# A fused four-layer graph network: layer 0's relu into a PSUM bank, compact means, and newly drawn instruction lists

## The chip, the cores and the metric

The kernel runs on one core of one Trainium2 chip. The time is that of one execution on the device, in microseconds (us), as the median of three runs. Five engines work side by side, each through its own queue in order: PE (TensorE, matmuls), DVE (VectorE), ACT (ScalarE), POOL (GpSimd) and SP (SyncE, which here only issues DMAs). They wait for each other by semaphores.

## What is computed

Four graph layers stand one behind the other, each with a layer norm and a relu ahead of it and a residual around it, for 128 graphs of 128 nodes with 256 features and one common adjacency matrix:

```python
h = jnp.maximum(_layernorm(x), 0.0)
x = x + _L0_gnn_ref(h, adj, W, b)          # deg * (h Wi' + b) + adj @ (h Wj')
h = jnp.maximum(_layernorm(x), 0.0)
x = x + _L1_gnn_ref(h, adj, W, a_src, a_dst)   # Wh, leaky-relu logits, masked softmax, attn @ Wh
h = jnp.maximum(_layernorm(x), 0.0)
x = x + _L2_gnn_ref(h, adj, W, a)          # as layer 1 with F1 = 128; out is [attn @ hW, hW]
h = jnp.maximum(_layernorm(x), 0.0)
x = x + _L3_gnn_ref(h, adj, Wq, bq, ...)   # 8-head masked attention and an output projection
```

In layers 1 and 2 a logit is e_src of one node plus e_dst of another; so each graph needs one column of 128 numbers (e_dst) as a row on all partitions.

## The kernel before, in words

Two graphs (a pair) are worked on at a time, 64 pairs in all, and everything of a pair stays on the chip. The kernel is a software pipeline, unrolled in full: each engine's function has a `step(t)` that lists its operations in a fixed order, and `LAG` gives for each operation by how many steps it runs behind. At step t an operation handles pair t - LAG. So `LAG`, together with the order of the `if due(...)` lines, is the whole schedule of an engine; within a step the order is the order of its queue. `BANKS` gives each matmul result one of the eight PSUM banks (2 KB per partition) and the operation that frees it; `bank_free` waits for whoever held that bank last by this order.

Products that need more than the fast format holds are made of a high and a low part: ACT rounds a tile (`..._hi`), DVE takes the difference (`..._lo`), and PE adds three products (L988 to L990). The operations that matter here:

- Layer 0. `xt` is the pair's x, transposed on the host and loaded by SP (L252). DVE makes mean and variance from x (`stats0`, `mv0`, L537, L551). SP writes the means to a small DRAM tensor (L259) and reads them back to all partitions (`mean_b`, L266); POOL subtracts them from xt (L380). ACT rounds the relu of that (`relu_difference_high`, L812), and DVE takes relu minus rounded (`relu_difference_low`, L591). PE multiplies (`project0`, L988 to L990), and multiplies by the adjacency (`aggregate`, L1024).
- Layer 1. POOL normalises (L388), PE transposes (`h1t`, L998), ACT and DVE make relu high and low (L803, L599), PE projects (`project1`), ACT copies the result (`wh`, L825). POOL gathers the e_dst column (`dst1`, L411), SP writes it (L278) and spreads it to all partitions (`db1`, L284). ACT's `sum_logits` (`z1`, L851) reads that row and writes leaky-relu logits into the upper half of bank 7; DVE masks (L609), ACT takes exps (L860), PE transposes (`e1t`, L1060), ACT copies (`at1`, L868), PE multiplies (`attend`, L1068).
- Layer 2 runs the same way with names that end in 2; its relu'd transpose is one copy (`relu_transposed2`, `ht2`, L831), its projection is `project2` (L1044) into `hh`, and its sum of logits (`z2`) uses the same bank 7. For the first four and last five pairs PE transposes the column in place of the DMAs.
- Layer 3: projections kt, qt, v, `scores` (L1105), exps (L882, four at a time), POOL's product with the inverse sums (L417), PE's transposes (L1113), ACT's copies (L890), `attend3` (L1125), and the output projection `project4`; DVE adds the residual (L675) and SP stores.

The places that the change and the prediction's steps touch:

```python
    "zz1": (7, "z1", ('nmax1',)),
    "zz2": (7, "z2", ('nmax2',)),
...
                act.wait_ge(row_in[i][p % 2], ((p - BY_TRANSPOSE[0]) // 2 + 1) * 16)   # sum_logits waits for the row's DMA
...
                passed(act, "h2t", p)                                                  # relu_transposed2
                passed(pe, "ht2", p)                                                   # project2
```

Of the kernel before, what the change touches and what calls it, by code (L numbers as in the profile page):

```python
# [13 lines left out]
P = 128  # L14
D = 256
# [32 lines left out]
    "m1": (1, "m1", ('mj_lo1', 't0_1')),  # L48
    "pt0": (3, "pt0", ('p3t_0',)),
    "x4b": (2, "x4_mm", ('x4',)),  # L50
    "m0": (5, "m0", ('mj_lo0', 't0_0')),
    "kt": (0, "kt_mm", ('kt',)),
    "d1": (4, "d1", ('z1',)),
    "at2": (6, "e2t", ('at2',)),
    "qt": (2, "qt_mm", ('qt',)),
# [1 line left out]
    "pt3": (0, "pt3", ('p3t_3',)),
    "x3b": (6, "x3_mm", ('x3',)),
    "h1t": (3, "h1t", ('h1t_lo',)),
    "hh": (2, "hh_mm", ('hh',)),  # L60
    "sc0": (4, "scores", ('nmax3_0',)),
    "sc1": (1, "scores", ('nmax3_1',)),
    "sc2": (5, "scores", ('nmax3_2',)),
    "sc3": (0, "scores", ('nmax3_3',)),
    "ot": (2, "ot_mm", ('ot_lo',)),
    "at1": (6, "e1t", ('at1',)),
    "h0t": (6, "h0t", ('d0s',)),
    "v": (3, "v_mm", ('v',)),
    "pt1": (6, "pt1", ('p3t_1',)),
    "x2b": (1, "x2_mm", ('x2',)),  # L70
    "x1b": (2, "s0", ('x1',)),
    "wh1": (5, "wh1_mm", ('wh1',)),
    "wh0": (3, "wh0_mm", ('wh0',)),
    "h3t": (0, "h3t", ('h3t_lo',)),
    "prep": (6, "products", ('w1_split',)),
    "pt2": (5, "pt2", ('p3t_2',)),
    "d2": (4, "d2", ('z2',)),
# [1154 lines left out]
```

## Time and profile before

| | |
|---|---|
| median of 3 runs (lowest, highest) | 1249.41 us (1247.36, 1253.91) |
| the profiled execution: time, span | 1256.04 us, 1254.0 us |
| PE, POOL, DVE, ACT busy | 1216.2, 1106.0, 1079.9, 1061.9 us |
| granted TensorE clock, mean | 0.996 |
| DMA | 86.76 MB, mean 69 GB/s |
| read from HBM, written | 66.92 MB, 17.02 MB |

Times in the profile are from the first instruction. Matmuls overlap each other, so a matmul's listed duration (0.28 us) is longer than the distance to the next one (0.12 us): distances between starts tell the pace. A wait is listed with the engine and line that waited, and behind the arrow with whoever released it. "PEld" is the load of a matmul's weights, which runs ahead of the matmul. With 64 pairs the first steps fill the pipeline and the last ones drain it.

### The profile page before, as it was taken

What the parts mean: (1) busy time and instruction counts of PE and PEld (TensorE: products, weight loads), DVE (VectorE), ACT (ScalarE), POOL (GpSimd) and SP (SyncE); (2) the same over time, 40 slices, a digit from 0 to 9 for tenths busy, and PEclk for the clock granted to TensorE, in tenths of its full rate; (3) what the DMA queues carried; (4) which work ended last, traced back from release to release, by engine and by line L of the source; (5) the groups of instructions that cost most, each with busy time, mean ns of one, the idle gap of its engine ahead of it and who ended that gap; (6) DMA issues with size and microseconds to landing.
All of it is one profiled execution on the core that took longest, in us unless ns stands there. A gap on an engine that the chain in (4) does not pass through costs nothing. (4 is left out here: it accounts for less than half of the span.)

```text
span 1254.0 us, 43654 instructions
## 1 busy us (share of the span) xinstructions
PE 1216.2 (97%) x12001; PEld 1117.9 (89%) x12001; DVE 1079.9 (86%) x5141; ACT 1061.9 (85%) x3911; POOL 1106.0 (88%) x1848
## 2 busy tenths in 40 slices
PE   7899999999999999999999999999999999999996
PEld 6689999999999889999999989999998999999996
DVE  5798988988988888988998988998988988988884
ACT  3578888898988888888998988898898898888996
POOL 5889989999999889999999989999999899998763
PEclk9999999999999999999999999999999999999999
DMA  6323434444443434435434444534435534431000
GB/s 181 83 48 48 82 60 75 82 66 69 83 65 69 82 57 77 77 66 74 82 64 71 79 60 78 81 59 76 79 64 74 83 57 78 80 55 31 19 20 35
DMA packets 97679, 86.76 MB, mean 69 GB/s; under 512 B 31649, under 2 KB 81313, under 8 KB 97441
## 3 DMA queue, kind: packets, MB, share of 16 engines
q1 hardware_dynamic: 94960, 82.26, 37.8%
q8 instruction: 102, 1.67, 0.6%
q14 instruction: 137, 1.11, 0.5%
q10 hardware_dynamic: 2480, 1.71, 0.5%
HBM read 66.92 MB, written 17.02 MB: 67 GB/s over the span
## 5 line engine op out<-in xcount | busy, mean ns | idle before, releaser
L882 ACT ACTIVATE exps<-masked,nmax 128x128 f32<-128x128 f32 x1024 | 397.0, 396 | 0.2 <-DVE nmax L652 0.2
L417 POOL TENSOR_TENSOR probs<-exps,rsum 128x512 f32<-128x512 f32 x256 | 274.8, 1075 | 22.1 <-DVE rsum L660 22.1
L652 DVE CUSTOM_DVE_ANT_0 masked<-bank,mask 128x128 f32<-128x128 f32 x1024 | 229.6, 285 | 11.4 <-ACT exps L882 7.3
L388 POOL TENSOR_SCALAR y<-x,nm,rstd 128x256 f32<-128x256 f32 x384 | 228.5, 604 | 1.9 <-issue 1.0
L882 ACT ACTIVATION_READ_ACCUMULATOR exps<-masked,nmax 128x1 f32 x1024 | 199.3, 195 | 0.0
L537 DVE BATCH_NORM_STATS2 stats<-x 128x6 f32<-128x256 f32 x512 | 188.6, 411 | 11.0 <-DMA x<-in_x 8.6
L365 POOL TENSOR_TENSOR rstd<-veps,power 128x2 f32<-128x2 f32 x256 | 183.1, 715 | 0.1
L988 PE MATMUL bank<-w_hi,ht_hi 128*128 128x512 f32 (+1 forms) x512 | 180.5, 352 | 0.9 <-DVE ht_lo L599 0.5
L989 PE MATMUL bank<-w_lo,ht_hi 128*128 128x512 f32 (+1 forms) x512 | 175.1, 342 | 0.0
L990 PE MATMUL bank<-w_hi,ht_lo 128*128 128x512 f32 (+1 forms) x512 | 174.8, 341 | 0.0
L1113 PE MATMUL bank<-ident,probs 128*128 128x128 f32 x1024 | 153.6, 273 | 0.3 <-ACT v L874 0.3
L890 ACT ACTIVATE probs3t<-bank 128x512 f32<-128x512 f32 x256 | 150.8, 590 | 2.4 <-PE bank L1113 2.3
L1113 PEld LDWEIGHTS bank<-ident,probs 128*128 128x128 f32 x1024 | 122.4, 142 | 8.7 <-issue 0.9
L998 PE MATMUL bank<-ident,y 128*128 128x128 f32 x768 | 116.6, 275 | 6.7 <-POOL y L388 6.7
L990 PEld LDWEIGHTS bank<-w_hi,ht_lo 128*128 128x128 f32 x512 | 97.0, 189 | 11.9
L988 PEld LDWEIGHTS bank<-w_hi,ht_hi 128*128 128x128 f32 x512 | 96.7, 189 | 11.3 <-DVE ht_lo L599 0.9
L989 PEld LDWEIGHTS bank<-w_lo,ht_hi 128*128 128x128 f32 x512 | 97.3, 190 | 9.3
L860 ACT ACTIVATE ez<-z,nmax 128x128 f32<-128x128 f32 x256 | 99.8, 395 | 2.2 <-DVE nmax L609 2.0
L998 PEld LDWEIGHTS bank<-ident,y 128*128 128x128 f32 x768 | 89.5, 142 | 9.1 <-POOL y L388 8.9
L380 POOL TENSOR_TENSOR xt_sb<-xt_sb,mean_b 128x512 f32<-128x512 f32 x62 | 96.9, 1562 | 0.0
L599 DVE SCALAR_TENSOR_TENSOR ht_lo<-bank,ht_hi 128x512 fp32r<-128x512 f32 x128 | 86.2, 673 | 11.2 <-ACT ht_hi L803 11.1
L825 ACT ACTIVATE wh<-bank 128x258 f32<-128x258 f32 x128 | 49.5, 387 | 50.4 <-PE bank L990 50.4
(129 smaller groups left out, 3904.9 us busy)
## 6 DMA issues: line engine op xcount, KB each, us to landing
x<-in_x SPq DMA_DIRECT2D x64, 256.0 KB, 5.7
xt_sb<-in_xt SPq DMA_DIRECT2D x64, 256.0 KB, 5.1
out<-x SPq DMA_DIRECT2D x64, 256.0 KB
mean_b<-rows SPq DMA_DIRECT2D x62, 256.0 KB, 4.4
db<-rows SPq DMA_DIRECT2D x110, 128.0 KB, 4.0
rows<-dst SPq DMA_DIRECT2D x110, 1.0 KB, 4.0
rows<-mv SPq DMA_DIRECT2D x62, 2.0 KB, 3.1
probs<-in_w0t ACTq DMA_DIRECT2D x1, 256.0 KB, 6.3
```

The lines of the kernel that those rows point to most:

```text
L365: pool.tensor_tensor(rstd[i][:, b], veps[i][:, b], power[:], ALU.pow).then_inc(S[f"rstd{i}"], 1)
L388: last = pool.tensor_scalar(y[i][:, b, g], src[:, bx, g], nm[i][:, s, g:g + 1], rstd[i][:, s, g:g + 1], ALU.add, ALU.mult)
L417: pool.tensor_tensor(probs3[:, p % BUFFERS["probs3"], j], exps3[:, p % BUFFERS["exps3"], j], rsum3[:, s, j].unsqueeze(2).to_broadcast([P, ...
L537: last = dve.bn_stats(stats[i][:, b, g], src[:, bx, g])
L652: last = dve.tensor_tensor_reduce(masked3[:, b, j, i], bank_of(f"sc{j}")[:, i * P:(i + 1) * P], mask[:], scale=-1.0, scalar=-MASKED, op0=A ...
L882: last = act.activation(exps3[:, b, j, i], masked3[:, p % BUFFERS["masked3"], j, i], ACT.Exp, bias=nmax3[:, s, j, i:i + 1], scale=-1.0, ac ...
L890: act.activation(probs3t[:, b, j].rearrange("p b n -> p (b n)"), bank_of(f"pt{j}")[:], ACT.Copy).then_inc(S[f"p3t_{j}"], 1)
L988: pe.matmul(out_ap, lhs[0], rhs[0], start=start, stop=False)
L989: pe.matmul(out_ap, lhs[0], rhs[1], start=False, stop=False)
L990: return pe.matmul(out_ap, lhs[1], rhs[0], start=False, stop=stop)
L998: last = pe.transpose(bank_of(f"h{i}t")[:, (c * G + g) * P:(c * G + g + 1) * P], y[i][:, b, g, c * P:(c + 1) * P], ident[:])
L1113: last = pe.transpose(bank_of(f"pt{j}")[:, i * P:(i + 1) * P], probs3[:, p % BUFFERS["probs3"], j, i], ident[:])
```

## The change

Four things are done.

1. **Layer 0's relu.** ACT writes the relu of the mean-free xt into bank 7 (new operation `h0r`), then copies that into `ht0_hi`, rounded; DVE subtracts the rounded part from the bank. So xt is read once, and its buffer is released by `h0r` alone. Bank 7 is shared in turn by `z1`, `h0r` and `z2`.
2. **The means.** `mv` holds the two graphs' means next to each other, and the two variances; only the means are written and spread, so the row is half as long, and POOL reads every second element instead of every fourth.
3. **Weights' semaphores.** Layer 3's weights for q, k and v count on one semaphore.
4. **The lists.** Order, lags and banks of all engines are drawn anew, with longer transfer times assumed.

```diff
 LAG = {
-       "adj_spread": -31, "m1": -6, "pt0": 1, "x4_mm": 2, "m0": -6, "kt_mm": -1, "d1": -4, "e2t": -2, "qt_mm": -1, "h2t": -3, "pt3": 1,
...
+       "adj_spread": -31, "pt0": 3, "pt3": 3, "d1": -2, "x3_mm": 0, "hh_mm": -1, "h1t": -3, "scores": 1, "ot_mm": 3, "h0t": -7, "v_mm": 1,
...
     "zz1": (7, "z1", ('nmax1',)),
+    "h0r": (7, "h0r", ('h0t_lo',)),
     "zz2": (7, "z2", ('nmax2',)),
...
-        mean_b = sb("mean_b", [P, 2, P * G * 2])
+        mean_b = sb("mean_b", [P, 2, P * G])
...
-        mv = [sb(f"mv{i}", [P, SMALL, G, 2]) for i in range(4)]
+        mv = [sb(f"mv{i}", [P, SMALL, 2, G]) for i in range(4)]
...
-                read_before(sp, "xt", p, "h0t_hi", "h0t_lo")
+                read_before(sp, "xt", p, "h0r")
...
-                sp.dma_start(rows[0][b], mv[0][:, p % SMALL].rearrange("p g s -> p (g s)")).then_inc(row_out[0][b], 16)
+                sp.dma_start(rows[0][b], mv[0][:, p % SMALL, 0]).then_inc(row_out[0][b], 16)
...
-                means = mean_b[:, bm].rearrange("p (n g s) -> p g n s", g=G, s=2)[:, :, :, 0]
+                means = mean_b[:, bm].rearrange("p (n g) -> p g n", g=G)
...
-                dve.scalar_tensor_tensor(ht0_r[1][:, b].rearrange("p c g n -> p (c g n)"), xt_sb[:, bx].rearrange("p c g n -> p (c g n)"), 0.0,
-                                         ht0_r[0][:, b].rearrange("p c g n -> p (c g n)").bitcast(F32),
-                                         ALU.max, ALU.subtract).then_inc(S["h0t_lo"], 1)
+                dve.tensor_tensor(ht0_r[1][:, b].rearrange("p c g n -> p (c g n)"), bank_of("h0r")[:],
+                                  ht0_r[0][:, b].rearrange("p c g n -> p (c g n)").bitcast(F32), ALU.subtract).then_inc(S["h0t_lo"], 1)
...
+            def relu_difference(p):
+                bx = p % BUFFERS["xt"]
...
+                bank_free(act, "h0r", p)
+                act.activation(bank_of("h0r")[:], xt_sb[:, bx].rearrange("p c g n -> p (c g n)"), ACT.Relu).then_inc(S["h0r"], 1)
+
+            def relu_difference_high(p):
+                b = p % BUFFERS["ht0"]
+                passed(act, "h0r", p)
                 read_before(act, "ht0", p, last_of("m0", "m1"))
-                act.activation(ht0_r[0][:, b].rearrange("p c g n -> p (c g n)"), xt_sb[:, bx].rearrange("p c g n -> p (c g n)"), ACT.Relu).then_inc(S["h0t_hi"], 1)
+                act.activation(ht0_r[0][:, b].rearrange("p c g n -> p (c g n)"), bank_of("h0r")[:], ACT.Copy).then_inc(S["h0t_hi"], 1)
```

Of the start, two moves: DVE's rounding of w0's low part (`w0_low`) now stands behind the first pair's subtraction of the means, and in the order within a step ACT's `exp3_2` now stands behind `mj_hi0`, not ahead of it.

**ACT, from the second copy of `wh` to `ht2`, in the middle of the program.** The row's sum of layer 1 is `bank7<-db1,wh`, that of layer 2 `bank7<-db2,hh`; `ht2` is layer 2's relu. Before, behind the second `wh` copy:

```order
L803 ACTIVATE ht3_hi<-bank0 128x512
L890 ACTIVATE probs3t<-bank5 128x512
L851 ACTIVATE bank7<-db2,hh 128x128 x2
L882 ACTIVATE exps3,ssum3<-masked3,nmax3 128x128 x4
L819 ACTIVATE mj_hi<-bank1,rstd0 128x256
L860 ACTIVATE ez2,ssum2<-z2,nmax2 128x128 x2
L882 ACTIVATE exps3,ssum3<-masked3,nmax3 128x128 x4
L819 ACTIVATE mj_hi<-bank5,rstd0 128x256
L868 ACTIVATE at2<-bank6 128x256
L890 ACTIVATE probs3t<-bank3 128x512
L851 ACTIVATE bank7<-db1,wh 128x128 x2
L831 ACTIVATE ht2<-bank1 128x512
```

Now, behind the second `wh` copy, first the eight that follow it:

```order
L886 ACTIVATE exps3,ssum3<-masked3,nmax3 128x128 x4
L878 ACTIVATE v<-bank6 128x512
L894 ACTIVATE probs3t<-bank4 128x512
L801 ACTIVATE ht3_hi<-bank5 128x512
L886 ACTIVATE exps3,ssum3<-masked3,nmax3 128x128 x4
L823 ACTIVATE mj_hi<-bank2,rstd0 128x256
L855 ACTIVATE bank7<-db2,hh 128x128 x2
L894 ACTIVATE probs3t<-bank1 128x512
```

and then the next nine:

```order
L864 ACTIVATE ez2,ssum2<-z2,nmax2 128x128 x2
L823 ACTIVATE mj_hi<-bank4,rstd0 128x256
L886 ACTIVATE exps3,ssum3<-masked3,nmax3 128x128 x4
L872 ACTIVATE at2<-bank3 128x256
L835 ACTIVATE ht2<-bank1 128x512
L894 ACTIVATE probs3t<-bank2 128x512
L894 ACTIVATE probs3t<-bank0 128x512
L855 ACTIVATE bank7<-db1,wh 128x128 x2
L841 ACTIVATE hh<-bank6 128x260
```

Layer 1's sum stood eleventh behind the copy and is now sixteenth; `ht2` stood behind that sum and is now ahead of it.

**PE, from layer 2's transposes to the scores** (`y2` is the input of those transposes, `hh,at2` is layer 2's attention, `w2_sb,ht2` is `project2`). Before:

```order
L990 MATMUL bank2<-ht3_hi,wq_lo 128x256
L998 MATMUL bank1<-ident,y2 128x128 x4
L1113 MATMUL bank0<-ident,probs3 128x128 x4
L1068 MATMUL bank6<-hh,at2 128x128 x2
L998 MATMUL bank3<-ident,y1 128x128 x4
L1044 MATMUL bank2<-w2_sb,ht2 128x130 x4
L1105 MATMUL bank4<-kt,qt 128x128
L1105 MATMUL bank1<-kt,qt 128x128
```

Now:

```order
L1066 MATMUL bank3<-ident,ez2 128x128 x2
L1004 MATMUL bank1<-ident,y2 128x128 x4
L1119 MATMUL bank2<-ident,probs3 128x128 x4
L1119 MATMUL bank0<-ident,probs3 128x128 x4
L1074 MATMUL bank3<-hh,at2 128x128 x2
L1050 MATMUL bank6<-w2_sb,ht2 128x130 x4
L1004 MATMUL bank0<-ident,y1 128x128 x4
L1111 MATMUL bank5<-kt,qt 128x128
```

The transposes of layer 2's exps (`ez2`) now stand directly ahead (before, twelve products of `qt` lay between them and `y2`), and of the two blocks between `y2` and `project2` the transposes of `y1` have given way to a second block of `probs3`.

**SP, one step of its nine DMAs.** Before:

```order
L252 DMA xt_sb<-in_xt 128x512
L284 DMA db2<-rows2 128x256
L266 DMA mean_b<-rows0 128x512
L278 DMA rows1<-dst1 128x2
L247 DMA x0<-in_x 128x2x256
L284 DMA db1<-rows1 128x256
L259 DMA rows0<-mv0 128x4
L278 DMA rows2<-dst2 128x2
L271 DMA out<-x4 128x2x256
```

Now:

```order
L253 DMA xt_sb<-in_xt 128x512
L285 DMA db2<-rows2 128x256
L279 DMA rows1<-dst1 128x2
L285 DMA db1<-rows1 128x256
L248 DMA x0<-in_x 128x2x256
L272 DMA out<-x4 128x2x256
L260 DMA rows0<-mv0 128x2
L267 DMA mean_b<-rows0 128x256
L279 DMA rows2<-dst2 128x2
```

Write and spread of layer 1's row (`rows1`, `db1`) and of the means (`rows0`, `mean_b`) now follow each other directly; the load of `x0` no longer stands between the first two.

## Rows read from the trace of the kernel before

**Rows 1.** Busy us by stretch: PE, PEld, DVE, ACT, POOL; clock, DMA share, GB/s.

```profile
620.41:638.86 18.45, 18.45 (x189) 17.20 (x187) 16.70 (x81) 16.54 (x62) 17.29 (x30) 1.00 0.44 75
112.30:1165.00 1052.70, 1042.95 (x10425) 963.43 (x10424) 933.95 (x4473) 924.05 (x3417) 965.02 (x1618) 1.00 0.42 70
1165.00:1240.00 75.00, 70.19 (x813) 65.83 (x815) 56.97 (x306) 68.85 (x274) 52.14 (x76) 1.00 0.07 23
```

**Rows 2.** Timeline of PE, the aggregation's first matmul: start us, duration us, instruction.

```profile
112.34 0.58 PE L1024 MATMUL bank<-mj_hi,aggr_r 128*128 128x512 f32 x1
...
620.41 0.58 PE L1024 MATMUL bank<-mj_hi,aggr_r 128*128 128x512 f32 x1
...
638.86 0.58 PE L1024 MATMUL bank<-mj_hi,aggr_r 128*128 128x512 f32 x1
...
1165.13 0.58 PE L1024 MATMUL bank<-mj_hi,aggr_r 128*128 128x512 f32 x1
...
L1024 PE MATMUL bank<-mj_hi,aggr_r 128*128 128x512 f32 x57 | 30.5, 535 | 0.0
```

**Rows 3.** Waits, 112.3 to 1165 us: engine, tile, line, releaser; us in all, times, longest.

```profile
PE bank L1044 <- ACT ht L831: 9.2, 18, 1.0
...
PEld bank L1044 <- ACT ht L831: 15.8, 28, 1.2
...
ACT bank L851 <- DMA db<-rows: 70.8, 92, 2.1
```

**Rows 4.** Timeline of PE around `project2`: a dense step, then a stretched one.

```profile
614.01 0.60 PE L998 MATMUL bank<-ident,y 128*128 128x128 f32 x4
614.44 1.06 PE L1044 MATMUL bank<-w_sb,ht 128*128 128x130 f32 x8
615.46 1.17 PE L1105 MATMUL bank<-kt,qt 32*128 32x128 f32 x32
...
726.19 0.60 PE L998 MATMUL bank<-ident,y 128*128 128x128 f32 x4
727.58 1.16 PE L1044 MATMUL bank<-w_sb,ht 128*128 128x130 f32 x8 [0.79 <-ACT ht L831]
728.72 1.05 PE L1105 MATMUL bank<-kt,qt 32*128 32x128 f32 x26
```

**Rows 5.** Timeline of ACT between the second wh copy and ht2, stretched step.

```profile
716.45 0.39 ACT L825 ACTIVATE wh<-bank 128x258 f32<-128x258 f32 x1 [0.34 <-PE bank L990]
...
723.91 0.59 ACT L890 ACTIVATE probs3t<-bank 128x512 f32<-128x512 f32 x1
726.34 0.67 ACT L851 ACTIVATE bank<-db,wh 128x128 f32<-128x128 f32 x2 [1.83 <-DMA db<-rows]
726.95 0.58 ACT L831 ACTIVATE ht<-bank 128x512 f32<-128x512 f32 x1
```

**Rows 6.** Groups of instructions by line and shape: busy us, mean ns, idle before.

```profile
L882 ACT ACTIVATE exps<-masked,nmax 128x128 f32<-128x128 f32 x1024 | 397.0, 396 | 0.2 <-DVE nmax L652 0.2
...
L890 ACT ACTIVATE probs3t<-bank 128x512 f32<-128x512 f32 x256 | 150.8, 590 | 2.4 <-PE bank L1113 2.3
...
L380 POOL TENSOR_TENSOR xt_sb<-xt_sb,mean_b 128x512 f32<-128x512 f32 x62 | 96.9, 1562 | 0.0
...
L803 ACT ACTIVATE ht_hi<-bank 128x512 fp32r<-128x512 f32 x128 | 75.7, 591 | 4.7 <-PE bank L998 1.4
...
L666 DVE TENSOR_TENSOR ot_lo<-bank,ot_hi 128x512 fp32r<-128x512 f32 x64 | 43.9, 686 | 6.2 <-ACT ot_hi L896 6.2
...
L812 ACT ACTIVATE ht_hi<-xt_sb 128x512 fp32r<-128x512 f32 x64 | 40.1, 626 | 3.3 <-DVE xt_sb L584 2.0 <-POOL xt_sb L380 1.4
...
L831 ACT ACTIVATE ht<-bank 128x512 f32<-128x512 f32 x64 | 37.3, 583 | 7.5 <-PE bank L998 7.3
```

**Rows 7.** Two lines by themselves: duration ns shortest/median/longest, first and last start.

```profile
L591 DVE SCALAR_TENSOR_TENSOR ht_lo<-xt_sb,ht_hi x64: 660/694/1247, 13.7 to 1146.9; 128x512 fp32r<-128x512 f32 x64
...
L417 POOL TENSOR_TENSOR probs<-exps,rsum x256: 1030/1040/1477, 80.1 to 1243.0; 128x512 f32<-128x512 f32 x128
```

More of the change, by code:

```diff
@@ L47 @@
     "prepa": (0, "adj_spread", ('adj_rows',)),
[L48 to L55, printed above, removed]
-    "h2t": (1, "h2t", ('ht2',)),
[L57 to L77, printed above, removed]
+    "pt0": (2, "pt0", ('p3t_0',)),
+    "pt3": (0, "pt3", ('p3t_3',)),
+    "d1": (5, "d1", ('z1',)),
+    "x3b": (3, "x3_mm", ('x3',)),
+    "hh": (6, "hh_mm", ('hh',)),
+    "h1t": (0, "h1t", ('h1t_lo',)),
+    "sc0": (5, "scores", ('nmax3_0',)),
+    "sc1": (4, "scores", ('nmax3_1',)),
+    "sc2": (2, "scores", ('nmax3_2',)),
+    "sc3": (1, "scores", ('nmax3_3',)),
+    "ot": (3, "ot_mm", ('ot_lo',)),
+    "h0t": (0, "h0t", ('d0s',)),
+    "v": (6, "v_mm", ('v',)),
+    "at1": (0, "e1t", ('at1',)),
+    "wh0": (4, "wh0_mm", ('wh0',)),
+    "wh1": (5, "wh1_mm", ('wh1',)),
+    "x2b": (0, "x2_mm", ('x2',)),
+    "pt2": (4, "pt2", ('p3t_2',)),
+    "x1b": (3, "s0", ('x1',)),
+    "h3t": (5, "h3t", ('h3t_lo',)),
+    "prep": (0, "products", ('w1_split',)),
+    "pt1": (1, "pt1", ('p3t_1',)),
+    "m1": (2, "m1", ('mj_lo1', 't0_1')),
+    "x4b": (6, "x4_mm", ('x4',)),
+    "d2": (0, "d2", ('z2',)),
+    "m0": (4, "m0", ('mj_lo0', 't0_0')),
+    "kt": (5, "kt_mm", ('kt',)),
+    "qt": (6, "qt_mm", ('qt',)),
+    "at2": (3, "e2t", ('at2',)),
+    "h2t": (1, "h2t", ('ht2',)),
     "zz1": (7, "z1", ('nmax1',)),
+    "h0r": (7, "h0r", ('h0t_lo',)),
     "zz2": (7, "z2", ('nmax2',)),
@@ L152, in gnn_kernel @@
         dst = [None] + [sb(f"dst{i}", [P, 2, G]) for i in (1, 2)]
-        mean_b = sb("mean_b", [P, 2, P * G * 2])
-        rows = [nc.dram_tensor(f"rows{i}", [2, P, G * 2 if i == 0 else G], F32).ap() for i in range(3)]
+        mean_b = sb("mean_b", [P, 2, P * G])
+        rows = [nc.dram_tensor(f"rows{i}", [2, P, G], F32).ap() for i in range(3)]
         row_out = [[sem(f"row{i}_out{b}") for b in range(2)] for i in range(3)]
@@ new lines, in step @@
+                if due(t, "rstd0") and t > LAG["rstd0"]:
+                    inverse_deviation(0, t - LAG["rstd0"])
+                if due(t, "dst2") and not at_an_end(t - LAG["dst2"]):
+                    gather_dst(2, hh, "hh", "hh", F1 + 1, t - LAG["dst2"])
+                if due(t, "d0") and t - LAG["d0"] >= MEANS_BY_TRANSPOSE:
+                    subtract_means(t - LAG["d0"])
+                if due(t, "p3_2"):
+                    normalise_p3(2, t - LAG["p3_2"])
+                if t == LAG["w3_low1"]:
+                    low_w3(1)
@@ new lines, in step @@
+                if due(t, "veps3"):
+                    shifted_variance(3, t - LAG["veps3"])
+                if due(t, "nm3"):
+                    negative_mean(3, "y3", t - LAG["nm3"])
+                if due(t, "rstd3"):
+                    inverse_deviation(3, t - LAG["rstd3"])
+                if due(t, "y3"):
+                    normalise(3, x3, t - LAG["y3"])
+                if due(t, "rsum1"):
+                    clear_empty_rows(t - LAG["rsum1"])
+                if due(t, "dst1") and not at_an_end(t - LAG["dst1"]):
+                    gather_dst(1, wh, "wh", last_of("wh0", "wh1"), D + 1, t - LAG["dst1"])
@@ new lines, in step @@
+                if due(t, "p3_0"):
+                    normalise_p3(0, t - LAG["p3_0"])
+                if due(t, "r0"):
+                    biased_x0(t - LAG["r0"])
+                if due(t, "p3_3"):
+                    normalise_p3(3, t - LAG["p3_3"])
+                if due(t, "veps0") and t > LAG["veps0"]:
+                    shifted_variance(0, t - LAG["veps0"])
+                if t == LAG["w3_low0"]:
+                    low_w3(0)
+                if t == LAG["w3_low3"]:
+                    low_w3(3)
@@ L680, in step @@
                     prepare_rows()
+                if due(t, "x4"):
+                    sum_x4(t - LAG["x4"])
+                if due(t, "nmax2"):
+                    mask_logits(2, mask2, t - LAG["nmax2"])
+                if due(t, "mv1"):
+                    mean_and_variance(1, t - LAG["mv1"])
+                if due(t, "stats0") and t > LAG["stats0"]:
+                    stats_of(0, x0, t - LAG["stats0"])
+                if t == LAG["w1_split"]:
+                    split_w1()
+                if due(t, "mv0") and t > LAG["mv0"]:
+                    mean_and_variance(0, t - LAG["mv0"])
@@ new lines, in step @@
+                if due(t, "d0s") and t - LAG["d0s"] < MEANS_BY_TRANSPOSE:
+                    subtract_first_means(t - LAG["d0s"])
+                if due(t, "mj_lo1"):
+                    low_mj(1, t - LAG["mj_lo1"])
+                if t == LAG["w0_low"]:
+                    low_w0()
+                if due(t, "t0_1"):
+                    add_own(1, t - LAG["t0_1"])
+                if due(t, "kt"):
+                    add_bias("kt", kt, bk_sb, 1.0, t - LAG["kt"])
+                if due(t, "rsum2"):
+                    inverse_sum(2, "rsum2", "x3", t - LAG["rsum2"])
@@ L791, in round_w3 @@
             def round_w3():
[L792 to L794 removed]
+                act.wait_ge(w3_in, 80)
                 act.wait_ge(wo_in, 48)
```

365 lines of the change are left out of this document (152 added, 213 removed), and 24 rows, old and new, of the table LAG.

## The prediction

> **What bounds the kernel now.** I read the busy time by stretches first. In one undisturbed step (one pair of graphs, 620.41 to 638.86 us) PE is busy all 18.45 us, POOL 17.29, DVE 16.70, ACT 16.54; the clock stands at 1.00 [rows 1]. So PE sets the step where nothing disturbs it, and POOL is next. Then I took the length of a step from PE's own order: the aggregation's first matmul stands once in every step. From 620.41 to 638.86 it is 18.45 us, but from 112.34 to 1165.13 us, 57 of them or 56 steps, it is 1052.79 / 56 = 18.80 [rows 2]. The reader should see 0.35 us per step that is not matmul work, 56 x 0.35 = 19.6 us in all.
>
> Next, the waits of that stretch say where. PE waits for one thing above all: `project2` (L1044) for the relu'd transpose ht2, which ACT makes at L831: 9.2 us by the matmuls, 15.8 us by the weight loads that go ahead of them. ACT itself waits longest at L851, the sum of logits, for the destination row that a DMA brings: 70.8 us in 92 waits [rows 3]. Two steps side by side join the two [rows 4]: in the dense one, `project2` starts 0.43 us after the transposes ahead of it and lasts 1.02 us until the scores; in the other it starts 1.39 us after them and lasts 1.14, 1.08 us lost. ACT's order in the same place tells why [rows 5]: the second `wh` copy ends at 716.84, the copy of probs3t ahead of the sum ends at 724.50, and the sum then stands 1.83 us for its row. The relu ht2 is the next in ACT's queue, and PE is waiting for it. The wait is layer 1's row; the one who pays is layer 2's projection, which only stands behind it.
>
> **The change, part by part.** Durations come from the profiled execution, 1256.04 us (span 1254.0 and some 2 us around it), which is 6.6 us above the median of the runs shown; since the stall hangs on when transfers land, I take that as a run with more of it, and the time without the stall as common to all.
>
> *The order on ACT.* Now ht2 stands three places ahead of layer 1's sum of logits, not behind it. That alone takes it out of the reach of the wait. The sum also stands later behind `wh`. Before, 724.50 - 716.84 = 7.66 us lie between [rows 5]. New between them are a group of four exps3 (397.0 / 256 = 1.55 us), two copies of probs3t (0.59 each), the copy of v (taken like those, 0.59) and ht2 (0.58) [rows 6]; nothing leaves. 7.66 + 3.90 = 11.6 us. The row of the step shown arrived 9.5 us after the copy (716.84 to 726.34), and that wait of 1.83 us is near the longest, 2.1 [rows 3, 5]; the worst trip was therefore 9.8. It now has 1.8 us to spare. Layer 2's sum moves the same way behind `hh`: exps3, h1t_hi and the new relu come in, one copy of probs3t goes out, 1.55 + 0.59 + 0.63 - 0.59 = 2.2 us at least, which covers its waits too. **The term: -19.6 us**, bounds 0 (the stall finds another place) and -19.6 (no more than all of it).
>
> *What is late next.* On PE, `project2` stands as far behind its transposes as it did. Layer 2's attention stands nearer to its transposed exps: three blocks of four transposes or so, 3 x 0.43 = 1.3 us [rows 4], in which ACT must make the copy at2; the nearest row, a copy out of PSUM twice as wide, takes 0.59 [rows 6], so 0.7 us are left. Layer 1's transposes also stand nearer to their projection, but blocks of 32, 32 and 12 matmuls still lie between, where the eight of `project2` take 1.02 us [rows 4]: room enough for a relu of 0.59 and a difference of about 0.69 [rows 6]. Each fits; I take 0.
>
> *The relu through PSUM.* ACT gains one instruction of 128x512 in each of 64 steps. Reading SBUF it takes 0.63 us (L812), from PSUM 0.58 to 0.59 (L831, L803) [rows 6]; one that reads SBUF and writes PSUM at this width is not in the trace. I take 0.63 for it, and the second becomes a copy out of PSUM at 0.59: ACT +0.59 us per step, bounds 0.5 and 0.7. From 16.54 this makes 17.1 of 18.45 [rows 1]: beside PE, cover 1.3 us per step. If that cover were gone, 56 x 0.59 = 33 us would show.
>
> *The low part.* DVE's difference reads the bank: 0.69 (like L666) in place of a median of 0.69 with outliers to 1.25 [rows 6, 7]; DVE has 1.75 us free per step, so 0.
>
> *The means side by side.* The row's DMA is half as large, and POOL's subtraction (L380, 1.56 us) reads its means from an 8-byte step instead of 16. Its bounds are 1.56 and the 1.04 of L417, POOL's nearest operation of that width [rows 6, 7]. PE waits for no POOL operation in the 1052.8 us [rows 3], so 0.
>
> *SP.* The same nine DMAs per step, in another order: the row write and the spread of layer 1 and of the means now stand next to each other, so SP stands through each landing. The large load of x no longer gets between layer 1's write and spread. The earlier release of xt (by the one relu) lets its load go sooner. I put 0 on it.
>
> *Start and end.* The first pair has one more relu ahead of its product (+0.6), but DVE no longer rounds w0's low part before the first subtraction. In the drain ACT carries one more exps3 group behind its last mj copy (+1.6); there ACT is busy 68.85 of 75 us [rows 1], so this may show. I take 0, with bounds of 4 either way.
>
> POOL's room has a second reason to grow. The low part's old form read two SBUF tiles (xt and ht0_hi). Its longest took 1247 ns against a shortest of 660, and POOL's product with the sums 1477 against 1040 [rows 7]; in layer 0's new form one of the two inputs comes from PSUM. The Trainium skill, SBUF — State Buffer, "Who interferes with whom", says that a DVE instruction with two SBUF inputs contends with a GpSimd instruction that reads SBUF, and that one with a single SBUF input does not. By that rule POOL gets its 0.4 us per step back and the rival below that has POOL as the bound loses ground; by the rows alone it would keep the chance of a 94% full engine. The sum is 1236 by either.
>
> **Sum.** 1256.04 - 19.6 + 0 = 1236.4, **1236 us**, 1.1% under the median of 1249.41. About 0.5%, 6.2 us, is what a measurement of this kernel can tell from no change.
>
> **The rivals.** *The stall moves in part.* The new order leaves 0.7 us for at2; if rows or relus come late there, PE loses at layer 2's attention what it gained at `project2`. For it: gaps on PE got shorter. Against: ACT has 1.3 us free per step, and nothing in its list ahead of at2 waits for a late DMA if the distances above hold. With half of the 19.6 us left, 1246 us.
>
> *ACT's ring, slower.* ACT now needs 17.1 of 18.45 us, and its queue is in order. Layer 2's sum of logits stands five places ahead of at2; if its row comes later than ACT's free 1.3 us and at2's 0.7 can take, 2.0 us together, in most steps, each step grows by what is over. At 0.5 us per step that is 56 x 0.5 = 28 us: 1264 us. For it: SP now stands through two landings per step ahead of that row's write, and the load of xt goes just ahead of its spread. Against: the distance grew by at least 2.2 us where the wait was at most 2.1 [rows 3].
>
> *POOL as the bound, also slower.* It has 18.45 - 17.29 = 1.16 us free and stands in order at the gathers of both rows. Only if its waits pass 1.16 us per step does it bind; 0.3 us more would cost 17 us, 1253 and so within the noise. I give it no case of its own and count it with the middle.
>
> *The order doesn't do it.* If the trips grow as the places do, because each spread stands behind another landing, the sum waits as before: 1249 to 1256 us.
>
> *More than forecast.* Start and drain shorten as well: under 1229 us.
>
> **How the numbers follow.** The forecast (1229 to 1243 us) gets 0.68: the one wait that PE shows has one cause, and both of its legs, the order and the distance, are changed. More than forecast gets 0.07; these two make faster 0.75. The stall in part (1243 to 1251) 0.11 and the order without effect (1249 to 1256) 0.04 make no change 0.15. ACT's ring gets 0.10. The range leaves out 2 in 10: most of "slower", and the far ends of the fast side: 1228 (forecast less the 4 of each end) to 1252 (past the half-kept stall, with the 6 us by which runs differ).
>
> **What would show it.** Right: the aggregation's first matmul every 18.4 to 18.5 us from the eighth on; no wait of PE for ht2; ACT's wait for the rows' DMA under 10 us in all; ACT busy some 38 us more; L417's counterpart without values near 1.47. A step over 18.6 with PE waiting for at2 or for `wh` shows the first two rivals; POOL without idle time, the third. The forecast is wrong if the mean step stays above 18.65.

## The result, and the profile after

The changed kernel takes 1275.58 us (median of 4 runs, 1269.76 to 1281.35) where the kernel before takes 1249.00 beside it: 1.0206 times as long, 95% interval 1.0146 to 1.0266. It is slower, by 1.5 to 2.7%, and outside the range of the forecast. Its profiled execution took 1272.41 us, with a span of 1270.4 against 1254.0; the granted clock is 0.996 in both.

First the page's busy times and one line of busy time by stretch (columns as in [rows 1]), from the eighth to the 63rd aggregation:

```profile
PE 1219.8 (96%) x12001; PEld 1112.8 (88%) x12001; DVE 1081.4 (85%) x5141; ACT 1089.3 (86%) x3975; POOL 1063.1 (84%) x1848
```

```profile
115.40:1164.30 1048.90, 1029.39 (x10238) 942.25 (x10236) 919.42 (x4397) 930.97 (x3412) 913.22 (x1594) 1.00 0.38 63
```

ACT has 27 us more work than before (1061.9), POOL 43 less (1106.0). The clock is 1.00 all through. So the work of these five explains no slower kernel; the step does. The aggregation's first matmul, now L1030, in PE's timeline:

```profile
115.42 0.48 PE L1030 MATMUL bank<-mj_hi,aggr_r 128*128 128x512 f32 x1
...
704.49 0.48 PE L1030 MATMUL bank<-mj_hi,aggr_r 128*128 128x512 f32 x1
...
724.95 0.48 PE L1030 MATMUL bank<-mj_hi,aggr_r 128*128 128x512 f32 x1
...
1164.30 0.48 PE L1030 MATMUL bank<-mj_hi,aggr_r 128*128 128x512 f32 x1
```

The shortest step is 18.41 us, as dense as before. But the mean of the 55 steps from the first of these rows to the last is (1164.30 - 115.42) / 55 = 19.07, where it was 18.80 over the same 55; the step in the middle rows takes 20.46. PE therefore loses 0.66 x 55 = 36 us. Of the 16.4 us between the two spans, 15.1 lie in these steps and 3.1 ahead of them; the drain gives back about 2.

The waits of that stretch, then those of SP over the whole run (engine, tile, line, releaser; us in all, times, longest):

```profile
ACT bank L855 <- DMA db<-rows: 82.5, 52, 4.1
DVE z L609 <- ACT bank L855: 72.5, 42, 3.9
...
PEld bank L1066 <- ACT ez L864: 15.4, 17, 2.1
...
PE bank L1066 <- ACT ez L864: 11.6, 13, 1.9
```

```profile
SPq L285 <- DMA rows<-dst: 403.7, 107, 7.1
SPq L267 <- DMA rows<-mv: 344.7, 62, 8.3
...
SPq L279 <- POOL dst L412: 17.3, 11, 2.8
```

PE's wait for ht2 [rows 3] is gone. In its place PE waits for layer 2's exponentials, which stand behind layer 2's sum of logits (L855). The sums of both layers wait 82.5 us in 52 waits for their rows, against 70.8 in 92 [rows 3]. By layer, over the 48 pairs from the ninth to the 56th, layer 1's sum now waits 3.9 us where it waited 36.2, and layer 2's 75.2 where it waited 28.4. So the loss is layer 2's. SP shows why. The same view of SP before had these two lines:

```profile
SPq L278 <- POOL dst L411: 424.6, 110, 9.7
...
SPq L266 <- DMA rows<-mv: 10.7, 7, 3.3
```

SP was ready at its row writes and waited for POOL's gathers (L278 there, L279 now). Now the gathers are ready before SP is, since it stands 344.7 us, 5.6 in each of 62 steps, at the landing of the means' row (L266, now L267). Worked out from the trace over the 55 steps, SP stands 13.1 us per step at landings, issues for 4.0 and waits for other engines for 1.2; before, these were 5.6, 3.9 and 8.4. Its own transfers thus take 17.1 us of a step of 19.07, against 9.5 of 18.80 before: SP's queue is nearly full.

One trip of layer 2's row, in the step from 704.49 to 724.95, in the timeline of all engines:

```profile
692.74 0.39 SPq L248 DMA_DIRECT2D x<-in_x  x1
693.17 0.46 SPq L272 DMA_DIRECT2D out<-x  x1
693.82 0.33 SPq L260 DMA_DIRECT2D rows<-mv  x1
...
697.87 0.36 ACT L841 ACTIVATE hh<-bank 128x260 f32<-128x260 f32 x1
698.30 0.18 POOL L412 COPY dst<-hh 128x2 f32<-128x2 f32 x1 [0.74 <-ACT hh L841]
...
701.81 0.33 SPq L267 DMA_DIRECT2D mean_b<-rows  x1
702.23 0.38 SPq L279 DMA_DIRECT2D rows<-dst  x1
...
707.39 0.32 SPq L285 DMA_DIRECT2D db<-rows  x1
...
711.98 0.68 ACT L855 ACTIVATE bank<-db,hh 128x128 f32<-128x128 f32 x2 [3.24 <-DMA db<-rows]
...
714.17 0.44 PE L1066 MATMUL bank<-ident,ez 128*128 128x128 f32 x2 [1.03 <-ACT ez L864]
```

POOL has gathered the row at 698.48. SP writes it at 702.23, because from 693.82 to 701.81 it stands through the landing of the means' row, which went out directly behind 512 KB of x and out. The sum then starts 3.24 us late, and PE pays 1.03 at once.

### The profile page after: what moved, and what is told of

Its sections match the earlier page's. It is cut to its first block and busy times, and to the rows that moved or that the text cites. A ratio compares the mean times of both kernels' runs of the same rounds, so it can differ in the third digit from the quotient of the medians.

```text
span 1270.4 us, 43726 instructions
## 1 busy us (share of the span) xinstructions
PE 1219.8 (96%) x12001; PEld 1112.8 (88%) x12001; DVE 1081.4 (85%) x5141; ACT 1089.3 (86%) x3975; POOL 1063.1 (84%) x1848
## 5 line engine op out<-in xcount | busy, mean ns | idle before, releaser
L418 POOL TENSOR_TENSOR probs<-exps,rsum 128x512 f32<-128x512 f32 x256 | 266.0, 1041 | 2.8 <-DVE rsum L660 2.8
L389 POOL TENSOR_SCALAR y<-x,nm,rstd 128x256 f32<-128x256 f32 x384 | 210.7, 556 | 23.1 <-issue 21.7
L994 PE MATMUL bank<-w_hi,ht_hi 128*128 128x512 f32 (+1 forms) x512 | 186.7, 365 | 3.1 <-DVE ht_lo L599 1.6
L1119 PE MATMUL bank<-ident,probs 128*128 128x128 f32 x1024 | 143.3, 273 | 2.9 <-DVE t L568 0.6
L894 ACT ACTIVATE probs3t<-bank 128x512 f32<-128x512 f32 x256 | 143.1, 587 | 2.8 <-PE bank L1119 2.8
L1119 PEld LDWEIGHTS bank<-ident,probs 128*128 128x128 f32 x1024 | 118.6, 141 | 13.3 <-issue 7.0
L609 DVE CUSTOM_DVE_ANT_0 z<-bank,mask 128x128 f32<-128x128 f32 x256 | 63.1, 285 | 75.7 <-ACT bank L855 75.6
L347 POOL TENSOR_SCALAR veps<-mv 128x2 f32<-128x2 f32 x256 | 56.8, 222 | 82.4 <-DVE mv L552 68.3
L864 ACT ACTIVATE ez<-z,nmax 128x128 f32<-128x128 f32 x256 | 100.7, 394 | 14.1 <-DVE nmax L609 10.7
L855 ACT ACTIVATE bank<-db,hh 128x128 f32<-128x128 f32 x110 | 37.3, 373 | 78.7 <-DMA db<-rows 78.6
```

The costliest lines, as they stand in the source:

```text
L389: last = pool.tensor_scalar(y[i][:, b, g], src[:, bx, g], nm[i][:, s, g:g + 1], rstd[i][:, s, g:g + 1], ALU.add, ALU.mult)
L418: pool.tensor_tensor(probs3[:, p % BUFFERS["probs3"], j], exps3[:, p % BUFFERS["exps3"], j], rsum3[:, s, j].unsqueeze(2).to_broadcast([P, ...
L894: act.activation(probs3t[:, b, j].rearrange("p b n -> p (b n)"), bank_of(f"pt{j}")[:], ACT.Copy).then_inc(S[f"p3t_{j}"], 1)
L994: pe.matmul(out_ap, lhs[0], rhs[0], start=start, stop=False)
L1119: last = pe.transpose(bank_of(f"pt{j}")[:, i * P:(i + 1) * P], probs3[:, p % BUFFERS["probs3"], j, i], ident[:])
```

## The experiments

The theory: SP's queue. It stands through the means' landing with layer 2's row behind it. The rivals: ACT's queue is too full with 27 us more work, or PE's new order leaves the copies at1 and at2 too little room. The experiments start from the changed kernel unless the text says otherwise. They fall into three sets, each on one chip, and the kernel before took 1272, 1292 and 1254 us there: a ratio holds within its set, and only ratios and steps are compared across sets.

| run | set | us, median | ratio to before (95%) | mean step, us |
|---|---|---|---|---|
| x1, layer 2's row ahead of the spread | 1 | 1236.71 | 0.9714 (0.9674 to 0.9754) | 18.43 |
| x2, the spread one step later | 1 | 1241.01 | 0.9742 (0.9703 to 0.9781) | 18.42 |
| x3, the write ahead of x and out | 1 | 1264.89 | 0.9936 (0.9911 to 0.9961) | 18.79 |
| x4, kernel before with the new SP list | 1 | 1254.28 | 0.9847 (0.9808 to 0.9887) | 18.68 |
| y1, kernel before | 2 | 1295.19 | 1.0024 (0.9996 to 1.0052) | 19.41 |
| y2, changed kernel | 2 | 1356.42 | 1.0480 (1.0439 to 1.0520) | 20.54 |
| y3, x1 with the old relu | 2 | 1242.36 | 0.9596 (0.9556 to 0.9637) | 18.46 |
| y4, kernel before, ht2 ahead of z1 | 2 | 1297.85 | 1.0028 (1.0003 to 1.0054) | 19.50 |
| z1, changed kernel | 3 | 1294.79 | 1.0324 (1.0289 to 1.0360) | 19.39 |
| z2, x1 again | 3 | 1241.36 | 0.9892 (0.9867 to 0.9916) | 18.42 |
| z3, x and out behind the rows | 3 | 1243.87 | 0.9914 (0.9885 to 0.9942) | 18.43 |
| z4, x1 with wide means | 3 | 1239.92 | 0.9886 (0.9859 to 0.9914) | 18.43 |

The second table is worked out from the traces: the mean trip of a row over the 48 pairs from the ninth to the 56th, in us, layer 1 / layer 2. "Held" is from the start of POOL's gather to the issue of the row's write, "write" from there to the issue of the spread, "spread" from there to the start of the sum of logits, "room" from the end of ACT's copy of wh or hh to that start. Where the sum waits for its row, "room" is the length of the trip; where it never waits (x1, z2), it is what ACT's list leaves. The trip itself, from the end of the copy to the landing of the spread, takes 8.65 / 8.62 us in the kernel before and 11.90 / 12.06 in the changed kernel (first profiles), 12.61 / 12.39 in z1, 8.29 / 8.08 in x1 and 7.86 / 7.88 in z2.

| run | held | write | spread | room |
|---|---|---|---|---|
| before, first profile | 0.21 / 0.21 | 4.21 / 4.34 | 4.15 / 4.04 | 8.68 / 8.65 |
| changed, first profile | 2.53 / 3.06 | 4.92 / 4.84 | 4.84 / 4.15 | 12.36 / 12.12 |
| x1 | 0.21 / 0.21 | 3.43 / 3.71 | 7.72 / 6.62 | 11.43 / 10.60 |
| x3 | 1.95 / 0.93 | 4.88 / 6.18 | 5.27 / 4.13 | 12.17 / 11.30 |
| x4 | 0.23 / 0.22 | 3.38 / 4.62 | 4.66 / 4.10 | 8.37 / 9.00 |
| y1, before | 0.21 / 0.21 | 4.67 / 4.69 | 4.32 / 4.00 | 9.32 / 8.97 |
| y2, changed | 3.77 / 3.71 | 5.52 / 5.09 | 4.84 / 4.41 | 14.21 / 13.27 |
| y4 | 0.21 / 0.21 | 4.57 / 4.60 | 4.59 / 4.14 | 9.44 / 9.01 |
| z1, changed | 2.97 / 3.43 | 5.11 / 4.73 | 4.76 / 4.22 | 12.90 / 12.43 |
| z3 | 0.46 / 0.21 | 4.02 / 4.63 | 6.91 / 5.69 | 11.46 / 10.60 |

### Where the means' spread stands (x1, x2, z1, z2)

x1 and z2 are one kernel, with two lines of SP's step exchanged:

```diff
                 if due(t, "row_out0") and t - LAG["row_out0"] >= MEANS_BY_TRANSPOSE:
                     write_means(t - LAG["row_out0"])
+                if due(t, "row_out2") and not at_an_end(t - LAG["row_out2"]):
+                    write_row(2, t - LAG["row_out2"])
                 if due(t, "row_in0") and t - LAG["row_in0"] >= MEANS_BY_TRANSPOSE:
                     spread_means(t - LAG["row_in0"])
-                if due(t, "row_out2") and not at_an_end(t - LAG["row_out2"]):
-                    write_row(2, t - LAG["row_out2"])
```

> Theory (SP's queue: the means' row is written behind two transfers of 256 KB and its spread stands directly behind it, so SP stands 6 to 8 us there with layer 2's row waiting behind): with layer 2's row written ahead of the means' spread, that row goes out as soon as POOL has gathered it, about 3 us sooner; ACT's wait for layer 2's row falls from 82 us to under 15, the dense stretch's mean step goes from 19.07 to about 18.5, time 1234 to 1245. Rival 1 (ACT's queue is too full since it has 27 us more work): ACT's work is unchanged, the waits only change their names, 1265 to 1280. Rival 2 (PE's new order leaves too little room for the copies at1 and at2): PE's waits for them stay, 1265 to 1280.

x2 puts the spread where the kernel before has it: `row_in0` from lag 7 to 8, and its two lines behind those of `row_in2`.

> Theory: the means' spread goes one step later, behind layer 2's spread, as in the kernel before; SP no longer stands through that landing, the row of layer 2 goes out when it is gathered: 1233 to 1243, ACT's wait for layer 2's row under 15 us. Its risk is POOL's subtraction waiting for means that come 5 us later; it has some 13 us to spare. Rivals 1 and 2: 1265 to 1280, as nothing but SP's order changes.

z1 and z2 put the changed kernel and x1 on one chip:

> The changed kernel, untouched, on the same chip as the kernel with layer 2's row ahead of the means' spread, so that both have one ratio to the kernel before. Theory: its distance from the copy of hh to layer 2's sum is 12 us or more, where the mended kernel, which never waits, shows 10.6; both rows stand 2.5 us or more behind their gathers; 1265 to 1360 us, by the chip.

> Layer 2's row ahead of the means' spread, again, beside the changed kernel. Theory: 1234 to 1245 on any chip, since its lists leave more room than a row's trip takes; mean step 18.4 to 18.5. If on a chip with longer landings it waits after all: over 1250.

All four came out in the theory's ranges: x1 1236.71, x2 1241.01, z2 1241.36 us, against 1294.79 for the changed kernel in z2's set, which is 4.1% less by an exchange of two lines. ACT, DVE, PE and POOL have the same lists in z1 and z2, so neither ACT's 27 us nor PE's order is what costs. z2's timeline in the same place:

```profile
676.62 0.33 SPq L260 DMA_DIRECT2D rows<-mv  x1
...
681.54 0.39 ACT L841 ACTIVATE hh<-bank 128x260 f32<-128x260 f32 x1
681.99 0.18 POOL L412 COPY dst<-hh 128x2 f32<-128x2 f32 x1 [0.31 <-ACT hh L841]
682.20 0.33 SPq L279 DMA_DIRECT2D rows<-dst  x1
682.62 0.38 SPq L267 DMA_DIRECT2D mean_b<-rows  x1
685.42 0.33 SPq L253 DMA_DIRECT2D xt_sb<-in_xt  x1
685.84 0.38 SPq L285 DMA_DIRECT2D db<-rows  x1
...
692.52 0.68 ACT L855 ACTIVATE bank<-db,hh 128x128 f32<-128x128 f32 x2
```

The row goes out 0.21 us after the gather began. The means' row still takes 5.2 us to land (from 676.62 to 681.79 by the trace), but SP spends that time waiting for the gather and not with a gathered row behind it, and the sum finds its row there: no bracket behind the row at 692.52. SP's waits in z2 have turned round again, beside those of the changed kernel above:

```profile
SPq L279 <- POOL dst L412: 367.5, 110, 5.4
SPq L285 <- DMA rows<-dst: 157.7, 61, 3.9
...
SPq L267 <- DMA rows<-mv: 21.4, 9, 3.7
```

### Why the means' row lands late (x3, z3)

x3 writes the means ahead of x and out; z3 issues x and out last of all. The order of SP's step in each, from `row_in1` on:

```diff
-load store row_out0 row_in0 row_out2
+row_out0 load store row_in0 row_out2
```

```diff
-load store row_out0 row_in0 row_out2
+row_out0 row_in0 row_out2 load store
```

> Asks why the landing of the means' row takes 6 to 8 us where it took 3.1. If it is because the write goes out behind the load of x and the store (512 KB in the same queue), then ahead of them it lands in 3 to 4 us, the spread follows 3 us sooner and most of the loss is gone: 1238 to 1252. If the landing is long for another reason (the row's shape, the traffic as a whole), SP stands 5 us or more there as before and the time stays at 1262 to 1278.

> The means' spread still stands directly behind its write, ahead of layer 2's row, but the load of x and the store are issued behind all three. If the means' row lands late because 512 KB go ahead of it in the queue: SP's time from write to spread falls from 6.4 to 7.2 us to 3 to 4, layer 2's row goes out within 1 us of its gather, 1236 to 1250. If standing through any landing at that place is what costs, however short: layer 2's row stays over 2 us late, 1260 or more.

x3 missed: 1264.89 us is in the range that I gave to another reason. But its table row tells a third story. Layer 2's row is held 0.93 us in place of about 3, and then its own write takes 6.18 where the changed kernel's takes 4.7 to 5.1, so the delay has changed its owner. A likely reason, which no run tests by itself, is that this write now goes out 4.7 us behind the 512 KB where it was 7.8 us (medians). z3 is clean. There the means' spread still stands directly behind its write, and SP stands through every landing:

```profile
SPq L285 <- DMA rows<-dst: 245.6, 89, 5.4
...
SPq L267 <- DMA rows<-mv: 173.0, 62, 4.6
SPq L279 <- POOL dst L412: 153.1, 95, 2.7
```

Each stand is 173.0 / 62 = 2.8 us against 362.8 / 62 = 5.9 for the changed kernel in the same set, layer 2's row is not held (0.21 us) and layer 1's hardly (0.46), and the kernel takes 1243.87. So the two halves of the cause can be separated: a spread directly behind its write costs SP one landing, and that landing is twice as long here behind 512 KB in the same queue. The Trainium skill, DMA: Bandwidth & Descriptors, "Queues, rings and completion order", says that each of the transfer engines consumes the descriptors of a queue in ring order; the 2.8 and 5.9 us agree with it. With either half taken away (x2 the first, z3 the second) PE keeps its 18.4 us; it takes both.

### The same list in the kernel before (x4)

SP's step in the order of the changed kernel, lags fitted to it, all else as before:

```diff
-loadt row_in2 row_in0 row_out1 load row_in1 row_out0 row_out2 store
+loadt row_in2 row_out1 row_in1 load store row_out0 row_in0 row_out2
-"row_in0": 9, "store": 18
+"row_in0": 8, "store": 19
```

> The kernel before with SP's list in the changed kernel's order and nothing else changed. Theory: the means' row now lands behind two large transfers there too and rows of layer 2 go out later; as POOL gathers that row later in the step than in the changed kernel, part of the wait is hidden: 1253 to 1270. Rival (SP's list has nothing to do with it): 1246 to 1252, no change.

The number falls in the theory's range and yet against it: beside it the kernel before took 1272.21, so x4 takes 1.5% less. The rival, no change, is wrong as well, as the interval leaves out 1. Its waits of SP:

```profile
SPq L284 <- DMA rows<-dst: 357.9, 110, 6.0
SPq L266 <- DMA rows<-mv: 239.3, 62, 5.7
SPq L278 <- POOL dst L411: 167.4, 97, 9.2
```

SP does stand at the means, 3.9 us per step. But here POOL gathers late enough that SP is back before it (it still waits 167.4 us for gathers, and holds rows 0.22), and layer 1's write, with no load of x between it and its spread any more, takes 3.38 us against 4.21 and 4.67 in the two profiles of the kernel before, on other chips. That the missing load is the reason is not shown: it is missing in the changed kernel as well, and there this write takes 4.92. So the list does no harm by itself in the kernel before. The harm must lie in how it meets POOL's and ACT's new lists, in which hh is ready while SP is still standing.

### ACT's order alone (y1, y2, y4)

As the kernel before had taken 1249 us at first and 1272 in set 1, both kernels ran untouched in set 2:

> The kernel before, untouched, since beside the first four experiments it took 1272 us where it had taken 1249. Two accounts: the chips differ in how long a small transfer takes to land, and this kernel, which waits for rows, shows it: then its waits for rows on ACT are well over the 71 us of the first profile and its mean step is over 19.0 where it takes 1272, and DMA medians are longer by some tenths of a us. Or something else is slower (clock, an engine): then the dense step itself is longer than 18.45 us.

> The changed kernel, untouched, beside the kernel before on the same chip. Theory (both kernels wait for rows; the changed one because SP stands for the means' row): it waits about as much as on the first chip, 1265 to 1290, so that the ratio to the kernel before can be anything from 1.00 to 1.02, by what the chip does to the other. Rival (a loss of the change that has nothing to do with landings): the ratio is 1.02 again.

The sets differ, and by the landings. Each set has its own chip, but no run separates the chip from the occasion. y1's shortest step is 18.35 us, so no engine is slower; but SP's waits for rows are 359.1 us in 109 where they were 315.5, ACT's wait for them 115.8 where it was 70.8, and PE's for ht2 34.1 where it was 9.2:

```profile
ACT bank L851 <- DMA db<-rows: 115.8, 103, 3.1
...
PE bank L1044 <- ACT ht L831: 34.1, 41, 2.3
```

The changed kernel suffers more from this than the kernel before does (1.048 here, 1.032 in set 3); my guess of 1.00 to 1.02 went the wrong way. Its trip for layer 2 exceeds the 10.60 us of room by 1.5, 1.8 and 2.7 us in the three profiles, and the mean step exceeds 18.41 by 0.66, 0.98 and 2.13.

y4 is the first leg of my main term, in the kernel before:

```diff
+                if due(t, "ht2"):
+                    relu_transposed2(t - LAG["ht2"])
                 if due(t, "z1"):
                     sum_logits(1, wh, "wh", D, t - LAG["z1"])
-                if due(t, "ht2"):
-                    relu_transposed2(t - LAG["ht2"])
```

> The kernel before with one change: ACT's relu ht2 ahead of layer 1's sum of logits. This is the first leg of my term of -19.6 us by itself. If PE's loss in the kernel before comes by that path alone: the mean step falls to under 18.6, 1.0 to 2.5 per cent faster than the kernel before beside it. If the stall only moves (the sum is as late as before and exp1, at1 come late): within 0.5 per cent.

The stall only moves. Waits of y4 from 112.3 to 1165 us:

```profile
DVE z L609 <- ACT bank L851: 55.5, 66, 2.0
PE bank L1105 <- DVE t L567: 50.2, 54, 2.2
ACT bank L851 <- DMA db<-rows: 43.3, 56, 2.2
...
ACT ht L831 <- PE bank L998: 39.7, 47, 1.0
```

PE no longer waits for ht2; it waits at the scores (L1105), 54 times, for t of layer 0, which frees one of their banks. DVE makes t in a queue that waits 55.5 us for the sums. No step is under 19.16 us. As long as the row's trip is as long as the room, whoever stands behind the sum pays, and this other order only picked another payer.

### The two parts that the title names (y3, z4)

y3 is x1 with the old relu: ACT and DVE both read xt, and SP's load of xt waits for both (`read_before(sp, "xt", p, "h0t_hi", "h0t_lo")`; `h0r` and its bank are gone). z4 is x1 with mean and variance interleaved as before.

> The changed kernel with layer 2's row ahead of the means' spread (1237 us) and the old relu of layer 0 (ACT and DVE both read the tile out of SBUF, the tile is freed by the later of the two). My term for the relu through PSUM was 0 on the path. If so: 1234 to 1242. If the earlier release of the tile is needed by SP (its load stands at the top of SP's step, ahead of layer 2's spread): SP stands there some us longer, 1245 to 1260. If the copy through PSUM costs ACT's queue: faster, under 1232.

> Layer 2's row ahead of the means' spread, with the means and variances interleaved as in the kernel before (rows of 2 KB, spread over 256 KB, POOL reads every fourth word). My term for the narrow layout was 0. If so: within 0.4 per cent of the kernel with the narrow layout, POOL's subtraction back at 1.56 us, its other operations unchanged. If the narrow row matters to the landings: SP's waits for rows grow by tens of us and the time by over 6 us.

Neither is worth much time here. y3 has a mean step of 18.46 us where x1, in another set, has 18.43; its 1242.36 us are 0.4 above the range for 0 and under that of the rival. SP does stand longer at the load of xt (207.8 us against 125.2 in x1), and layer 2's write takes 5.89 us from issue to spread; that is 2.2 more than x1's 3.71, and x1 had about as much to spare, 2.2 to 2.6 (6.62 behind the spread, where a sum that waits starts after 4.0 to 4.4). z4 takes 1239.92 us, the narrow layout 1241.36 in the same set. POOL's subtraction in z4, with wide means:

```profile
L381 POOL TENSOR_TENSOR xt_sb<-xt_sb,mean_b 128x512 f32<-128x512 f32 x62 | 97.0, 1564 | 0.2 <-issue 0.2
```

## Why the prediction was wrong

**What bounds the kernel: right.** PE's dense step of 18.45 us, and the 0.35 us above it from waits for rows [rows 2, 3]. x1 and z2 show what is left without them: 18.43 and 18.42.

**The failing step is "SP. ... I put 0 on it."** I had written what happens, "SP stands through each landing", and did not ask who is queued behind it. Layer 2's write is: it was held 3.06 us, and layer 1's, behind the next landing, 2.53. With three landings stood through one after the other, 6.4 + 4.8 + 4.9 us from write to spread, and the issues of the other DMAs between, SP's transfers alone take 17.1 us of a step of 19.07. My reason for 0, that the load of x no longer gets between layer 1's write and spread, does not help: that write takes 4.92 us in the changed kernel and 4.21 before. A sum over SP's queue was missing, though the rows of before would not have given its size. The kernel before waits 10.7 us in 7 waits, at most 3.3, for the means' landing because 11 us of other work lie between write and spread, and no row write of it directly follows 512 KB. Its landings, 3.2 + 4.3 + 4.2 us, and 3.9 us of issues make 15.6 us, which would have fitted into a step.

**The distances were right, the trip was not.** I worked out 11.6 us for layer 1's room and 2.2 us more than before for layer 2's, which on the 8.65 of the table would be 10.9; the kernels that never wait show 11.43 and 10.60. I set the first against the worst trip of before, 9.8 us, and the second against the longest wait, 2.1. The change made the mean trip 11.9 and 12.1 us. A distance had been compared with a length that the same change lengthens. For layer 1 it was still nearly enough (3.9 us of waits in 48 pairs), for layer 2 it was not (75.2). My rival "The order doesn't do it" said just that of the trips, but stopped at no change.

**The term of -19.6 us had one leg too many.** By y4 the order of ht2 and the sum is worth nothing by itself (1.0028). What gives the time back must then be the room, alone or with the order; no run has the room with ht2 behind the sum. With SP's order mended the 1236 us that I had forecast appear, 1236.71 in x1 and 1241.36 in z2.

**The rival that came true.** "ACT's ring, slower" had the right place, layer 2's sum ahead of at2, and the right cause, SP in two landings ahead of that row's write. It had a chance of 0.10 because I counted only the 2.2 us by which the room grew. Its price of 28 us was mis-sized: PE lost 36 in the profiled run, 54 in z1 and 117 in y2 (the excess over 18.41 times 55). Its cover was mis-sized too. Over the 48 pairs ACT waits 75, 98 and 144 us for layer 2's row in these three profiles, 1.57, 2.04 and 3.00 per pair, and the mean step exceeds 18.41 by 0.66, 0.98 and 2.13: about 1 us is covered, where I had counted 2.0.

**The small terms held.** ACT's relu into PSUM takes 0.58 us where I took 0.63; the pair adds 0.58 + 0.59 - 0.63 = 0.54 us per step, within my bounds of 0.5 and 0.7. ACT's whole busy time grew by 27 us, not 38; between y3 and z2, which differ in this one instruction, it is 1101.0 - 1069.0 = 32 us. DVE's difference is 0.69. POOL's subtraction takes 1.30, within 1.04 and 1.56. Start and end moved by 3.1 and about -2, within 4. The two relu instructions:

```profile
L816 ACT ACTIVATE ht_hi<-bank 128x512 fp32r<-128x512 f32 x64 | 37.7, 589 | 0.1
L810 ACT ACTIVATE bank<-xt_sb 128x512 f32<-128x512 f32 x64 | 37.2, 581 | 1.9 <-DVE xt_sb L585 1.9
```

**POOL's room grew, and mostly by the relu's form.** L417's long values [rows 7] are gone in the changed kernel, as I expected of an input that moved to PSUM. They are gone in y3 as well, where DVE reads two SBUF tiles as before (L591). But there another instruction of POOL pays: its tiny product with `has_any`, L357 in y3, which is L358 in the changed kernel. The first two lines are y3's, the third the changed kernel's (ns, shortest/median/longest):

```profile
L417 POOL TENSOR_TENSOR probs<-exps,rsum x256: 1032/1041/1055, 95.3 to 1229.6; 128x512 f32<-128x512 f32 x128
...
L357 POOL TENSOR_TENSOR rsum<-rsum,has_any x64: 186/662/752, 40.3 to 1183.7; 128x2 f32<-128x2 f32 x64
...
L358 POOL TENSOR_TENSOR rsum<-rsum,has_any x64: 187/195/201, 39.6 to 1212.5; 128x2 f32<-128x2 f32 x64
```

In y3 the 53 of these products that overlap L591 take 661 ns in the mean, the 11 others 186 to 200. That makes 25 us. In the kernel before the 21 of L417 that overlap L591 take 1469 ns against 1040, and the 59 of y that overlap it 862 against 557: 9 + 18 = 27 us. The rest of the 43 us by which POOL has less work is its subtraction, 62 x 0.26 = 16. So a new order only chose which instruction of POOL pays, and the one-input form took the loss away: POOL is busy 1091.2 us in y3 and 1063.3 in z2, which differ in the relu alone. The Trainium skill, SBUF — State Buffer, "Who interferes with whom", says that a DVE instruction with two SBUF inputs contends with a GpSimd instruction that reads SBUF; the trace agrees. L591 itself loses less: 813 ns in the mean for the 20 beside L417 and y, 700 for the 53 beside y and the tiny product, 691 for one beside nothing. My 0.4 us per step came out, 27 / 64 = 0.42, in part by luck: I had read it from one long value of L417, which has only 9 of the 27 us.

## What to carry to other kernels

A queue that issues transfers in order is an engine with waits of its own: when a change sets a read of DRAM directly behind the write that it depends on, the price is a whole landing for everything queued behind it (2.8 us here, and 5.9 with 512 KB issued just ahead). Add up the landings that a queue stands through and its issues, and set the sum against the step, as for any engine. Write the small rows that are ready ahead of the spread that has to wait, and issue large transfers where no small one follows; either was enough here. Before setting a longer room against a trip, work out the trip again under the new order; and ask of a wait that an order seems to cause whether another instruction would not pay it instead.

x1, two lines away from the changed kernel, takes less time than both: 0.9714 and 0.9892 times the kernel before in its two sets, with PE at its dense step.

## What the runs showed of the hardware that I had not expected

- How long a row of 1 KB takes to land depends on what else was issued to its queue just ahead of it. From the issue of the means' write to that of its spread it takes 3.4 us in z3 and 6.8 in z1, on one chip; SP stands 2.8 and 5.9 us of that. Twice is no fixed price: in x4 the same 512 KB stand ahead of a row of 2 KB, and SP stands 3.9 us.
- The chip, or the occasion, matters to a kernel that waits for landings. The kernel before took 1249, 1272, 1292 and 1254 us in four sets, with the same dense step (18.36 and 18.35 us in two profiles); layer 1's row takes 4.21 us from write to spread in one and 4.67 in the other. x1, which never waits, took 1236.71 and 1241.36 in two sets.
- ACT reads SBUF and writes PSUM in 581 ns (L810), where the same relu from SBUF to SBUF, which also rounds, takes 626 [rows 6].
- POOL's subtraction depends on the step at which it reads its broadcast means: 1.30 us with words 8 bytes apart, 1.56 with 16 (z4), the same width and the same count. The Trainium skill, GPSIMD Engine Reference, "Performance pitfalls for Q7 kernels", is on kernels for that engine's cores and puts a limit at 8 bytes and a price of 50% per element above it; here the whole instruction, one of whose two inputs has that step, takes 20% more.
